# Attention in 64-row tiles of TensorE: values split by keys, bias parts split by shifts, and one bias addition per unit on VectorE instead of three

## The reference, cut to what matters

```python
# first attention
bias = tisa_bias(kernel_offsets, kernel_amplitudes, kernel_sharpness, l)   # depends on i - j only
logits = jnp.einsum('bhld,bhmd->bhlm', q, k) * scale + bias[None]
attn = jax.nn.softmax(logits, axis=-1)
out = jnp.einsum('bhlm,bhmd->bhld', attn, v)
# attention of the second block: the same without a bias
attn = jnp.einsum('bhnd,bhmd->bhnm', q, k) * (1.0 / np.sqrt(DK))
attn = jax.nn.softmax(attn, axis=-1)
y = jnp.einsum('bhnm,bhmd->bhnd', attn, v)
```

## Time and profile before

| | value |
|---|---|
| median of 3 runs | 913.6 us |
| the profiled execution | 909.28 us |
| its span, first to last instruction | 907.4 us |
| stage 0 (about 52.0 to 470.7 us of the span) | 418.7 us |
| stage 1 (about 470.7 to 793.5 us) | 322.8 us |
| the rest behind it (maxima, experts, output) | 113.9 us |
| TensorE busy | 807.3 us, 89% |
| VectorE busy | 752.4 us, 83% |
| ScalarE busy | 636.9 us, 70% |

### The profile page before, as it was taken

One profiled execution on the slowest core, in us unless ns is written; L12 is line 12 of the kernel. 1 busy time (PEld: TensorE's weight loads), 2 busy tenths in 40 slices (PEclk: granted clock), 3 DMA queues, 4 the chain that ended last, 5 costly groups with the idle time before them and its releaser, 6 DMA issues.

```text
span 907.4 us, 22092 instructions
## 1 busy us (share of the span) xinstructions
PE 807.3 (89%) x8629; PEld 302.8 (33%) x8629; DVE 752.4 (83%) x1196; ACT 636.9 (70%) x1266; POOL 242.8 (27%) x548
## 2 busy tenths in 40 slices
PE   4289999999999999999999999999999999954950
PEld 2023333333333333333332223322232322244950
DVE  5589877989999998879999998899999899236735
ACT  6037777777776777777778988899989899921311
POOL 4110423200000405322300552342101301004773
PEclk9569999999999999999999999999999999966985
DMA  3655534655556445445313343232312121101313
GB/s 99 202 166 177 171 109 155 195 166 164 165 171 191 134 152 174 132 156 178 107 54 107 109 126 92 79 110 73 96 54 61 55 90 49 32 9 50 51 51 100
DMA packets 69469, 104.67 MB, mean 115 GB/s; under 512 B 15845, under 2 KB 45861, under 8 KB 69365
## 3 DMA queue, kind: packets, MB, share of 16 engines
q1 hardware_dynamic: 62805, 68.31, 25.8%
q10 hardware_dynamic: 5088, 31.92, 9.9%
q0 software_dynamic: 1472, 3.02, 1.5%
HBM read 84.19 MB, written 18.87 MB: 114 GB/s over the span
## 4 chain that ended last, share of the span: by engine, by line
PE 68%; DVE 9%; POOL 6%; DMA 5%; issue 4%; ACT 4%; SPq 2%; POOLq 0%; DVEq 0%
PE bank L1286 23%; PE bank L1305 20%; PE bank L1312 12%; PE bank L1266 7%; DVE unit_max L1003 4%; ACT prob_mem L901 4%; POOL prob_mem L791 3%; POOL moe_out L797 2%; DMA maxima_rows<-max_rows 2%; PE bank L1349 2%; PE bank L1239 2%; DVE stats L946 1%; PE bank L1234 1%; DMA q_rows<-maxima_rows 1%; DMA bias_parts<-prob_mem 1%
## 5 line engine op out<-in xcount | busy, mean ns | idle before, releaser
L901 ACT ACTIVATE prob_mem<-bank 128x512 f32<-128x512 f32 x1024 | 556.7, 597 | 140.2 <-PE bank L1312 116.5
L1266 PE MATMUL bank<-k_rows,q_rows 56*128 56x512 bf16 x1024 | 326.3, 392 | 20.9 <-DMA k_rows<-k_parts 12.4
L1305 PE MATMUL bank<-q_rows,k_rows 59*128 59x512 bf16 x1024 | 332.6, 386 | 6.2 <-DMA q_rows<-maxima_rows 2.3
L999 DVE CUSTOM_DVE_ANT_1 no_use<-bank,w_moe 128x1024 bf16<-128x1024 f32 x256 | 305.7, 1219 | 31.7 <-PE bank L1266 29.3
L1286 PE MATMUL bank<-prob_mem,v_ring 128*32 128x256 f32 x4096 | 320.5, 386 | 7.7 <-issue 6.6
L1003 DVE TENSOR_REDUCE unit_max<-bank 128x1 f32<-128x1024 f32 x256 | 297.3, 1216 | 16.3 <-PE bank L1266 14.7
L702 POOL CAST max_parts<-unit_max 128x8 bf16<-128x8 f32 x64 | 12.3, 192 | 557.4 <-DVE unit_max L999 315.2
L1305 PEld LDWEIGHTS bank<-q_rows,k_rows 59*128 59x128 bf16 x1024 | 80.9, 93 | 236.7 <-issue 109.5
L1286 PEld LDWEIGHTS bank<-prob_mem,v_ring 128*32 128x32 f32 x4096 | 102.6, 109 | 152.8 <-ACT prob_mem L901 62.6
L1312 PE MATMUL bank<-skew_mem,pick 96*32 96x512 bf16 x1664 | 138.2, 389 | 0.0
L1010 DVE TENSOR_TENSOR bank<-bank,w_moe 128x512 f32<-128x512 f32 x96 | 67.0, 698 | 25.0 <-PE bank L1305 24.7
(11 more groups left out here) (177 smaller groups left out, 526.9 us busy)
## 6 DMA issues: line engine op xcount, KB each, us to landing
w_moe<-bias_rows ACTq DMA_DIRECT2D x31, 960.0 KB, 5.4
q_rows<-q_parts SPq DMA_DIRECT2D x252, 48.0 KB
k_rows<-k_parts SPq DMA_DIRECT2D x126, 96.0 KB
skew_mem<-bias_parts SPq DMA_DIRECT2D x32, 378.0 KB, 4.4
unit_sums<-o_ring SPq DMA_DIRECT2D x63, 128.0 KB, 2.3
w_moe<-in_L_ffn_w_dram SPq DMA_DIRECT2D x16, 256.0 KB, 3.0
q_parts<-prob_mem SPq DMA_DIRECT2D x8, 384.0 KB, 3.1
k_parts<-prob_mem SPq DMA_DIRECT2D x24, 128.0 KB, 2.7
```

Source lines behind the costliest of these rows:

```text
L901: nc.scalar.activation(prob[:, kb, half * N:(half + 1) * N], b_bank(("exp", exp_no(n, kb, half))), ACT.Exp).then_inc(exp_done, 1)
L999: nc.vector.tensor_tensor_reduce(out=no_use[:, qb % 2, :].rearrange("p (k c) -> p k c", k=QB), in0=scores.rearrange("p (k c) -> p k c", k= ...
L1266: return nc.tensor.matmul(sa_slot(QB * m + qb)[:, f, :], q_rows[rows, m % SLOTS, qb * P:(qb + 1) * P], k_rows[rows, m % SLOTS, f * N:(f + ...
L1305: return nc.tensor.matmul(b_bank(("exp", exp_no(n, kb, f))), k_rows[rows, n % SLOTS, kb * P:(kb + 1) * P], q_rows[rows, n % SLOTS, f * N:( ...
```

## The change

The values and the bias matmuls go from tiles of 128 rows to tiles of 64 rows. `weigh_v` becomes `weigh_lower` (keys 0 to 63 of the block, rows 0 to 63 of the array) and `weigh_upper` (keys 64 to 127), four 64x32 matmuls each. The bias parts are laid out as two groups of 16 shifts, at partitions 0 to 47 and 64 to 111; `bias_half` adds one group, again with four 64x32 matmuls. The maxima are turned in two halves as well. TensorE now waits for itself by new semaphores, because both halves write the same bank: `av_lower`, `av_upper`, `bias_lower` and `max_t_lower`. VectorE adds the bias in one half block of a unit (`kb == 4`) instead of three. The loads of `skew` become two of 48 rows instead of one of 96, and `pick` is built by six selects on GpSimd instead of three. The order of the loop body is new.

```diff
@@ setup
-        pick = sb("pick", [96, 32], bf16)
+        pick = sb("pick", [HP + SR, VM], bf16)
...
@@ 
         def by_dve(n, kb, f):
-            return stage_of(n) == 0 and f == 1 and kb in (1, 4, 7)
+            return stage_of(n) == 0 and f == 1 and kb == 4
...
@@ 
-            src = bass.AP(row.tensor, row.offset, [[1, 32], [2 * L, 3], [1, SKW]])
-            queue.dma_start(skew[0:96, n % 3, 0:SKW], src).then_inc(skew_loaded[n % 3], 16)
+            for g in range(2):
+                src = bass.AP(row.tensor, row.offset + SHIFTS * g, [[1, SHIFTS], [2 * L, 3], [1, SKW]])
+                queue.dma_start(skew[g * HP:g * HP + SR, n % 3, 0:SKW], src).then_inc(skew_loaded[n % 3], 16)
...
@@ TensorE, helpers
-            def weigh_v(n, kb):
-
+            def weigh_half(n, kb, g):
+
+                rows = slice(g * HP, (g + 1) * HP)
                 for c in range(4):
-                    ins = nc.tensor.matmul(AV[VM * c:VM * (c + 1), :], v_ring[:, n % 4, kb, :],
-                                           prob[:, kb, c * W:(c + 1) * W], start=(kb == 0), stop=(kb == QB - 1),
-                                           tile_position=(0, VM * c))
+                    ins = nc.tensor.matmul(AV[VM * c:VM * (c + 1), :], v_ring[rows, n % 4, kb, :],
+                                           prob[rows, kb, c * W:(c + 1) * W], start=(kb == 0 and g == 0), stop=(kb == QB - 1 and g == 1),
+                                           tile_position=(g * HP, VM * c))
+                return ins
+
+            def weigh_lower(n, kb):
+
+                pe.wait_ge(exp_done, 2 * (QB * n + kb) + 2)
+                if kb == 0:
+                    pe.wait_ge(v_ready, n + 1)
+                    if n:
+                        pe.wait_ge(o_ready, n)
+                else:
+                    pe.wait_ge(av_upper, (QB - 1) * n + kb)
+                weigh_half(n, kb, 0).then_inc(av_lower, 1)
+
+            def weigh_upper(n, kb):
+
+                pe.wait_ge(av_lower, QB * n + kb + 1)
+                weigh_half(n, kb, 1).then_inc(av_done if kb == QB - 1 else av_upper, 1)
...
+            def bias_half(n, kb, f, g):
+
+                rows = slice(g * HP, g * HP + SR)
                 for c in range(4):
-                    at = f * N - kb * P + 32 * c + L - P
-                    ins = nc.tensor.matmul(b_bank(("exp", exp_no(n, kb, f)))[32 * c:32 * (c + 1), :], pick[:], skew[0:96, n % 3, at:at + N],
-                                           start=False, stop=True, tile_position=(0, 32 * c))
-                ins.then_inc(sb_done, 1)
+                    at = f * N - kb * P + VM * c + L - P
+                    ins = nc.tensor.matmul(b_bank(("exp", exp_no(n, kb, f)))[VM * c:VM * (c + 1), :], pick[rows, :],
+                                           skew[rows, n % 3, at:at + N], start=(f == 1 and g == 0), stop=(g == 1),
+                                           tile_position=(g * HP, VM * c))
+                ins.then_inc(sb_done[f] if g else bias_lower, 1)
+
+            def lower_added(n, kb, f):
+                i = exp_no(n, kb, f) + 1
+                pe.wait_ge(bias_lower, i - dve_before[i])
...
@@ TensorE, body of the loop over n and kb
+                    if pe_adds(n, kb, 1):
+                        b_bank_free(second)
+                        bias_half(n, kb, 1, 0)
+                    if pe_adds(n, kb, 0):
+                        lower_added(n, kb, 0)
+                        bias_half(n, kb, 0, 1)
                     if m < NU:
-                        ins.then_inc(sa_done, 1)
-                    if stage_of(n) == 0:
-                        for f in range(2):
-                            if not by_dve(n, kb, f):
-                                bias_b(n, kb, f)
...
+                        sa_free(QB * m + kb)
+                        scores_a(m, kb, 0)
+                    if pe_adds(n, kb, 1):
+                        lower_added(n, kb, 1)
                     else:
...
+                        b_bank_free(second)
+                    scores_b(n, kb, 1)
+                    if kb == 2:
+                        first_half(then[0], then[1])
+                    elif value[0] >= 0:
+                        weigh_lower(value[0], value[1])
+                    if pe_adds(n, kb, 1):
+                        bias_half(n, kb, 1, 1)
+                    if m < NU:
+                        scores_a(m, kb, 1)
+                    if kb == 2:
+                        weigh_lower(value[0], value[1])
+                    elif then[0] < NU:
+                        first_half(then[0], then[1])
...
+                    if then[0] < U:
+                        bias_half(then[0], then[1], 0, 0)
+                    if value[0] >= 0:
+                        weigh_upper(value[0], value[1])
+                    if turned_max:
+                        maxima_upper(n + 1)
```

More of the change, by code:

```diff
@@ L246, in sandwich_kernel @@
         tab_loaded = [sem(f"tab_loaded{s}") for s in range(4)]
-        sa_done = sem("sa_done")
+        sa_done = [sem(f"sa_done{f}") for f in range(2)]
         max_done = sem("max_done")
-        sb_done = sem("sb_done")
+        sb_done = [sem(f"sb_done{f}") for f in range(2)]
+        bias_lower = sem("bias_lower")
         raw_done = sem("raw_done")
@@ L404, in max_t @@
         def max_t(n):
-            return b_bank(("max", n))[0:3 * QB, 0:P // 2].bitcast(bf16)
+            return b_bank(("max", n))[0:3 * QB, 0:P]
         def exp_no(n, kb, f):
@@ L899, in _ @@
                         else:
-                            act.wait_ge(sb_done, i + 1 - dve_before[i + 1])
+                            act.wait_ge(sb_done[half], QB * n + kb + 1 - (dve_before[i + 1] if half else 0))
                         nc.scalar.activation(prob[:, kb, half * N:(half + 1) * N],
@@ L989, in block_max @@
             def block_max(m, qb):
-                dve.wait_ge(sa_done, QB * m + qb + 1)
+                for f in range(2):
+                    dve.wait_ge(sa_done[f], QB * m + qb + 1)
                 scores = sa_slot(QB * m + qb).rearrange("p a n -> p (a n)")
@@ L1265, in scores_a @@
                 rows = slice(f * HP, f * HP + KR)
-                return nc.tensor.matmul(sa_slot(QB * m + qb)[:, f, :], q_rows[rows, m % SLOTS, qb * P:(qb + 1) * P],
-                                        k_rows[rows, m % SLOTS, f * N:(f + 1) * N], start=True, stop=True)
+                nc.tensor.matmul(sa_slot(QB * m + qb)[:, f, :], q_rows[rows, m % SLOTS, qb * P:(qb + 1) * P],
+                                 k_rows[rows, m % SLOTS, f * N:(f + 1) * N], start=True, stop=True).then_inc(sa_done[f], 1)
             def sa_free(i):
@@ new lines, in weigh_upper, with maxima_half, maxima_lower @@
+            def weigh_upper(n, kb):
+                pe.wait_ge(av_lower, QB * n + kb + 1)
+                weigh_half(n, kb, 1).then_inc(av_done if kb == QB - 1 else av_upper, 1)
+            def maxima_half(n, g):
+                rows = slice(g * HP, (g + 1) * HP)
+                return nc.tensor.matmul(max_t(n)[:, rows], max_parts[rows, n % 2, :], ident_b[rows, rows], start=True, stop=True,
+                                        tile_position=(g * HP, 0))
+            def maxima_lower(n):
@@ L1301, in b_bank_free, with pe_adds @@
                     pe.wait_ge(free[0], free[1])
+            def pe_adds(n, kb, f):
+                return stage_of(n) == 0 and not by_dve(n, kb, f)
             def scores_b(n, kb, f):
                 rows = slice(f * HP, f * HP + KR + 3)
-                return nc.tensor.matmul(b_bank(("exp", exp_no(n, kb, f))), k_rows[rows, n % SLOTS, kb * P:(kb + 1) * P],
-                                        q_rows[rows, n % SLOTS, f * N:(f + 1) * N],
-                                        start=True, stop=(stage_of(n) == 1 or by_dve(n, kb, f)))
@@ L1309, in bias_b @@
-            def bias_b(n, kb, f):
-                for c in range(4):
-                    at = f * N - kb * P + 32 * c + L - P
-                    ins = nc.tensor.matmul(b_bank(("exp", exp_no(n, kb, f)))[32 * c:32 * (c + 1), :], pick[:], skew[0:96, n % 3, at:at + N],
-                                           start=False, stop=True, tile_position=(0, 32 * c))
-                ins.then_inc(sb_done, 1)
+                added = pe_adds(n, kb, f)
+                ins = nc.tensor.matmul(b_bank(("exp", exp_no(n, kb, f))), k_rows[rows, n % SLOTS, kb * P:(kb + 1) * P],
+                                       q_rows[rows, n % SLOTS, f * N:(f + 1) * N], start=not (added and f == 1), stop=not added)
@@ L1411, in _ @@
-                    if kb == MAX_AT and n + 1 < NU:
+                    then = divmod(QB * n + kb + 1, QB)
+                    value = (n, kb - 2) if kb >= 2 else (n - 1, kb + 6)
+                    second = ("exp", exp_no(n, kb, 1))
+                    if pe_adds(n, kb, 1):
[4 more added lines that the diff above has]
+                        bias_half(n, kb, 0, 1)
```

76 lines of the change are left out of this document (37 added, 39 removed).

## The result

The changed kernel takes 1989.91 us (median of 4 runs, 1989.12 to 1991.05) against 913.73 us before (4 runs, 911.34 to 915.63): 2.178 times the time, 95% interval 2.173 to 2.183. The prediction was slower, at 1195 us, with a range up to 1240. The direction was right and the size far off: the measured time lies 795 us above the prediction and 750 us above the top of the range.

A forecast was written before the change was run, and what follows sets the result against it. TensorE bounds stage 0; three engines are near the end in stage 1. 907.4 + 144 + 160 - 20 = 1191.4 us of span; with 1.9 for the execution and 4 for the median, 1195 us was predicted, range 935 to 1240.

The forecast's parts named there:

- What bounds the kernel: Stage 0: TensorE busy 12.16 of 12.25 us per unit; stage 1: TensorE, VectorE and ScalarE all near the end.
- The price of a change of shape: On TensorE, 0.10 us per change of tile shape, width alone included, taken as a wait of the whole array.
- Rivals 1, 2 and 3: Price within one array half, about 1035 us, 0.22; width change free, about 945, 0.10; same with self-waits hidden, about 893, 0.08.
- The groups: TensorE's queue in equal-width groups: 2.00 us per key block in stage 0, 1.78 in stage 1; units 16.8 and 14.3 us.
- the sum: Whole kernel: 907.4 us plus 144 for stage 0 and 160 for stage 1, less 20, giving 1191.4 us of span.
- the lower edge: With 0.21 per set, 0.43 for values, 0.09 per change: key blocks of 1.88 and 1.64, about 55 us less.
- TensorE's wait for itself: Between values lower and values upper, a releaser of about 0.05 us; covered in stage 1 outside `kb == 2`.
- VectorE's share: Taking 64 additions, 45 us, from VectorE brings nothing: it has slack in stage 0 and does not end last afterwards.
- At a granted clock of 0.99 and 1.00, which is the level of 2.4 GHz: Clock read in the earlier trace's windows of stage 0 and stage 1.
- something else: Remaining case, such as a lower clock in a TensorE that now waits more; chance 0.04.
- -20: Side work in both attention stages partly swallowed by longer key blocks: 20 us less, taken from between 0 and 53.

The follow-up runs named there:

- the run with four changes of shape: Kernel before, with half 0's bias right behind half 0's scores: four changes of tile width per stage 0 key block, not two; 946.2 us, ratio 1.037.
- the burst run: Changed kernel with 120 additional 128x128 matmuls in a row at one place of units 10, 20, 38 and 52; 1810.85 us in one run.

## Why the prediction was wrong, point by point

- **What bounds the kernel.** Right: TensorE ends last in stage 0; in stage 1 it, VectorE and ScalarE are close. The changed kernel's idle ScalarE and VectorE both wait for TensorE in both stages.
- **The price of a change of shape, and over which part of the array.** Right. 0.10 us was read from the earlier trace rows and from the earlier trace rows for a change of width alone; the run with four changes of shape gives 0.11 for each, and the timeline of the changed kernel shows that nothing of another width starts while a half streams. Rivals 1, 2 and 3 all fall on that. The Trainium skill, TensorEngine Tiling (Array Packing), Key Properties, has the rule that a change of mode drains the engine. The traces here agree, with 64x32 and 64x128 as two modes: 0.10 to 0.11 us for each change, and no overlap.
- **The groups.** Right to 0.1 us: 16.8 and 14.3 us per unit were reckoned, 16.76 and 14.44 measured at 2.4 GHz. That part of the slowdown is (16.76 - 12.25) x 32 + (14.44 - 9.26) x 32 = 310 us, where the sum had 304. Two slips did no harm: the lower edge, with 0.21, 0.43 and 0.09, is 1.85 us per key block of stage 0 and some 74 us less in all, not 1.88 and 55; and the 1.64 us of the earlier trace rows held the wait for ScalarE. TensorE's wait for itself was put at 0.05 us; the run with the values halves alone shows 0.09.
- **VectorE's share.** Right that it brings nothing; the part alone costs 4 us.
- **"At a granted clock of 0.99 and 1.00, which is the level of 2.4 GHz".** This is the step that failed: the term for a lower clock was put at nothing. The sum took every duration from rows at 2.4 GHz and gave the lower clock a place in the 0.04 for "something else", with no price. At the clock that was granted, a quiet unit takes 29.41 and 24.83 us: (29.41 - 16.76) x 32 + (24.83 - 14.44) x 32 = 737 us. With the 310 that makes 1047 of the 1080 us by which the span grew; the remaining 33, from side work, the start and the last units, were not taken apart; the sum had -20 there.
- **Why the clock.** The kernel before enters the loop at 0.5 as well and gets out of it within its first unit. The changed kernel does not get out. The values halves, which leave half of the array's rows idle, are enough to cause this. Alone in the kernel before they keep both stages at 0.5; four changes of shape alone do not; and in stage 1 the changed queue holds the clock once the values use all rows. For stage 0 they are not the whole account. It stays at 0.5 with the values whole too, and with the values on full rows it needed ten units to rise. So the bias halves, or the changes of shape around them, have a share that was not separated. What exactly the chip counts was not tried and stays open.

The trace of before had a hint that I read past. The second and third digits of its clock line are 5 and 6, so the loop starts at the low clock and leaves it only then; of a change that halves the filled part of the array in the values one could ask whether it still would. The price was to be had too, from the first key block of the loop in the kernel before:

```profile
52.95 1.05 PE L1312 MATMUL bank<-skew_mem,pick 96*32 96x512 bf16 x8
53.93 0.60 PE L1305 MATMUL bank<-q_rows,k_rows 59*128 59x512 bf16 x1
```

Two sets of 512 columns and a change of shape take 0.98 us there, against 0.54 at 2.4 GHz, so a set costs 0.22 us more. In the changed kernel a unit has 58 sets one behind the other in stage 0 (seven a key block and two more in `kb == 2`) and 48 in stage 1 (six a key block). That makes 12.8 and 10.6 us, where 12.65 and 10.39 were measured.

## What to carry to other kernels

In a kernel like this one, two row halves run side by side only while both hold work of the same tile width; so lay the queue out in groups of equal shape and charge about 0.1 us at each border (no run here shows a split that pays). Before reckoning with durations at 2.4 GHz, ask whether the loop enters at the low clock and whether the new work, array half empty, still raises it: here that was worth more than twice the visible cost. A cheap test on the chip is a burst of full matmuls: the units behind it show the speed at the high clock, and how long it lasts shows how well this work holds it.

## What the runs showed of the hardware that was not expected

- TensorE was 99% busy by the records over both attention stages and still granted 0.50, in one stretch of 1860 us of the profiled run. The mean clock was 0.519 in each of the four runs.
- Doubling the arithmetic made the kernel faster: 1593 us with the values on all rows, twice, against 1990 with each half once.
- The changed queue held 2.4 GHz for 171 us between the first two bursts of the burst run and 54 us more behind the second, and for 24 and 51 us from the start of the rise at the later two, with TensorE busy for 96% or more of each of these stretches. The Trainium skill, TensorE: Matmul & The Clock Gate, Part 1, describes a hardware block that sets the clock by how busy the engine has been recently. Busy by the records is not enough for that here: TensorE was busy for 99% of both stages and was granted 0.50.
- A wait of TensorE for its own matmuls: with the values halves alone the upper values start 0.09 us behind the recorded end of the lower ones. In the changed kernel a 64x32 set behind scores starts 0.51 to 0.56 us after them, self-wait or not (913 of 915 in the profile), so outside `kb == 2` the wait hardly ever ends last.
